# A routed, recurrent, routed block on one core: the second routing scatters its rows into slots, and the recurrence's rotations move to VectorE

## The chip, the cores and the metric

One core of a Trainium2 chip runs the whole program. The metric is the device time of one execution in microseconds, given as the median of several runs. The engines that matter are TensorE (PE, with PEld for its weight loads), VectorE (DVE), ScalarE (ACT), GpSimd (POOL) and the queue of SyncE (SP), which only issues transfers here.

## The reference, cut to what matters

```python
# x: [8, 512, 128] float32, that is T = 4096 tokens of D = 128
def moe(tokens, gate_w, w1, w2):          # E = 8 experts, F = 512, CAP = 160
    probs = softmax(tokens @ gate_w)
    e = argmax(probs)                     # one expert for each token
    pos = rank of the token among those of its expert, in token order
    # tokens with pos >= CAP are dropped: they get 0 from this layer
    out[t] = probs[t, e] * (relu(tokens[t] @ w1[e]) @ w2[e])
x = x + 0.5 * moe(layernorm(x), ...)
u = layernorm(x)                          # per batch: 512 steps of a linear recurrence
Bu = u @ B_w.T
h[t] = ifft(lambda * fft(h[t-1])).real + Bu[t]     # lambda from a_params, |lambda| = 1
x = x + h @ C_w.T + D * u
x = x + 0.5 * moe(layernorm(x), ...)      # same weights, routed anew
```

Token order runs over all batches, so the rank of a token in the second routing is known only once everything ahead of it has been routed.

## The kernel before, in words

The token tiles are 128 rows wide: NT = 32 tiles, TB = 4 of them for each of the NB = 8 batches. The experts have E * CAP = 1280 slots in all, held as NS = 10 tiles of 128 slots. The program has five stages.

1. **First routing** (`mark(0, 0)`, `rank(0, 0)`, `make_hot(0, 0)`, `place(0, 0)`, `index(0)`). VectorE picks the expert of each token and counts within a tile (`mark`). TensorE turns counts into ranks over all tokens (`rank`). VectorE makes slot numbers from them and one-hot tables of each slot number's two parts (`make_hot`). TensorE multiplies these tables, so that each slot gets the number of its token (`place`), and VectorE writes the list `tok` (`index`). GpSimd then gathers rows of x by `tok`, ten indirect transfers (`gather`, L317).
2. **Experts** (`slots(0)`). The steps are written out by hand in `pe_steps`, `dve_steps` and `act_steps`: i takes a slot tile in, u and d are the up and down products of an expert, o turns a row tile back, and x are small products that do nothing but run TensorE. GpSimd scatters the ten result tiles to `x1_dram` (`scatter`, L326).
3. **Recurrence** (L697 to L786 on VectorE, L972 to L1036 on TensorE). SP loads x1 batch by batch. A batch is split into groups of four steps. For batch b: VectorE's `stats` and `shift` and ScalarE's `deviation` and `normalise` make u, TensorE turns it (`turn_u`, L977), ScalarE copies it out (`copy_uT`), and TensorE sums each group (`group_sums`, L986). Then the sums are rotated back, added up along time and rotated forth. The rotation needs both halves of the 128 state rows exchanged, and before the change three engines share it: ScalarE copies the halves crosswise (`turned_part`, L419 and L420), GpSimd multiplies them (vb, L339), VectorE multiplies the plain part (va, L722), adds up (`carry`, z, L730) and makes zs in two half-height instructions (L734), while GpSimd makes zc (L344). `turn_forth` adds both to `state`. TensorE's `within_groups` and `read_out` make y, and VectorE's `add_back` and `gate_back` make x2 and its gate logits. The order on TensorE in turn i is `group_sums(i)`, `turn_u(i + 1)`, `read_out(i - 1)`, `within_groups(i)`.
4. **Second routing**, in three pieces of 3, 3 and 2 batches. The first piece's work stands within the recurrence, from turn 3 on, and the rest after it. SP stores x2 to `out` batch by batch (L278). When `index(1)` has written `tok`, and all stores have landed, GpSimd gathers rows of `out` by it.
5. **Experts again** (`slots(1)`), with the same steps, and ten scatters to `out`.

Engines meet through semaphores, each engine runs its own instructions in order, and a wait holds up everything behind it on that engine.

## Time and profile before

| | |
|---|---|
| runs | 176.22, 178.87, 179.49 us, median 178.87 |
| profiled execution, first to last instruction (span) | 175.4 us |
| the profiled execution's own time beside its span | not listed apart; the lowest of the runs is 0.8 us above the span |
| TensorE | 140.6 us busy (80%), mean granted clock 0.913 |
| VectorE | 89.4 us (51%) |
| ScalarE | 58.1 us (33%) |
| GpSimd | 52.8 us (30%), 80 instructions |
| stage 1, to the first gather | 0 to 27.8 us |
| stage 2, to the first statistics on x1 | 27.8 to 65.7 us |
| stage 3, to the last turn's `gate_back` | 65.7 to 120.0 us |
| stage 4, to the first gather's issue | 120.0 to 136.8 us |
| stage 5, to the end of the span | 136.8 to 175.4 us |

Busy shares are averages over these stages. The rows further down are of four kinds: the chain of waits (what released what, followed back from the end), timelines (start in us, length in us, engine, line, operation, tiles, and in square brackets the idle time ahead of it and who ended that), rows of one source line (how many, and the least, median and greatest length in ns), and windows (busy time of each engine in a stretch, and PEclk, the granted TensorE clock, where 1.00 is 2.4 GHz and 0.50 is 1.2 GHz). A timeline merges neighbouring instructions of one line: x4 means four.

### The profile page before, as it was taken

The page shows a single profiled execution, that of the slowest core. Times are in us where ns is not written, and L with a number is a line of the kernel's source. Part 1 is how long each engine was busy: PE and PEld are TensorE (multiplying, and loading weights), DVE is VectorE, ACT ScalarE, POOL GpSimd, SP SyncE. Part 2 cuts the span into 40 slices and gives each one's busy share as a digit, 9 for nine tenths or more (in the row PEclk, how much of TensorE's full clock was granted, in tenths as well). Part 3 has the DMA queues.
Part 4 walks back from the last instruction along what each step waited for, and adds up shares of the span by engine and source line. Part 5 has one row for each costly group of instructions (what it writes and reads, how often), then busy time and mean ns, then how long its engine had stood idle before and what let it go on. Part 6 is the DMA issues. An engine that isn't in the chain of part 4 may idle for free.

```text
span 175.4 us, 2538 instructions
## 1 busy us (share of the span) xinstructions
PE 140.6 (80%) x791; PEld 108.6 (62%) x791; DVE 89.4 (51%) x396; ACT 58.1 (33%) x144; POOL 52.8 (30%) x80
## 2 busy tenths in 40 slices
PE   6879999989999767599669669697169789999930
PEld 3138497489998322488558558586044269999820
DVE  1069763983583206067458588677754134235320
ACT  3421414554734003753643642610000021483200
POOL 2700005772067700022112112210000677105771
PEclk9997897999999999879999999999656965999996
DMA  4999990111011149000110110111010111000110
GB/s 133 330 366 359 371 551 19 57 48 30 0 36 45 62 133 336 28 2 0 60 60 0 64 60 0 62 60 64 0 60 0 30 45 51 23 4 28 49 45 30
DMA packets 11308, 16.21 MB, mean 92 GB/s; under 512 B 1664, under 2 KB 6272, under 8 KB 11264
## 3 DMA queue, kind: packets, MB, share of 16 engines
q1 hardware_dynamic: 9504, 13.11, 21.3%
q0 software_dynamic: 1280, 2.62, 5.0%
q10 hardware_dynamic: 512, 0.33, 0.7%
q8 instruction: 6, 0.10, 0.2%
q14 instruction: 6, 0.05, 0.1%
HBM read 12.65 MB, written 5.51 MB: 104 GB/s over the span
## 4 chain that ended last, share of the span: by engine, by line
PE 41%; DVE 22%; issue 11%; ACT 8%; DMA 8%; POOL 5%; SPq 1%; POOLq 1%; DVEq 0%; ACTq 0%
PE pair L910 12%; PE pair L921 10%; ACT u L440 5%; PE pair L852 4%; DVE sstat L701 4%; PE pair L879 4%; DMA xt<-x_turned 3%; PE pair L804 3%; PE pair L899 2%; DVE x L748 2%; POOL zc L344 2%; DVE smv L706 2%; DVE z L730 2%; DMA x<-x_scratch 2%; DMA xg<-out,tok 1%
## 5 line engine op out<-in xcount | busy, mean ns | idle before, releaser
L804 PE MATMUL pair<-warm_in,ones_bf 128*128 128x512 bf16 x80 | 22.3, 428 | 3.9 <-DMA x<-x_scratch 1.7
L910 PE MATMUL pair<-xcT,w1s 128*128 128x160 f32 x128 | 22.5, 323 | 0.0
L921 PE MATMUL pair<-hT,w2s 128*128 128x160 f32 x128 | 21.4, 312 | 0.8 <-ACT hT L394 0.8
L910 PEld LDWEIGHTS pair<-xcT,w1s 128*128 128x128 f32 x128 | 19.7, 206 | 0.9 <-ACT xcT L386 0.8
L921 PEld LDWEIGHTS pair<-hT,w2s 128*128 128x128 f32 x128 | 18.8, 199 | 1.5 <-ACT hT L394 0.8
L394 ACT ACTIVATE hT<-pair 128x320 f32<-128x320 f32 x32 | 13.7, 435 | 17.1 <-PE pair L910 15.8
L440 ACT ACTIVATE u<-x,snb,srs 128x128 f32<-128x128 f32 x32 | 13.1, 481 | 13.4 <-DVE snb L716 13.4
L804 PEld LDWEIGHTS pair<-warm_in,ones_bf 128*128 128x128 bf16 x80 | 8.3, 110 | 13.9 <-issue 3.3
L317 POOL DMA_INDIRECT xg<-x,tok x10 | 10.2, 1017 | 21.5 <-DVE tok L638 18.8
L317 POOL DMA_INDIRECT xg<-out,tok x10 | 10.1, 1006 | 20.9 <-DVE tok L638 18.2
L339 POOL TENSOR_TENSOR vb<-vq,st 128x128 f32<-128x128 f32 x8 | 3.6, 455 | 39.5 <-ACT vq L420 39.5
L386 ACT COPY xcT<-pair 128x128 f32<-128x128 f32 x20 | 4.9, 266 | 30.0 <-PE pair L894 30.0
L977 PE MATMUL pair<-ce,u 128*128 128x128 f32 x32 | 5.7, 305 | 10.6 <-ACT u L440 10.4
L326 POOL DMA_INDIRECT out<-xnew,tok x10 | 9.9, 985 | 12.4 <-DVE xnew L682 10.5
L326 POOL DMA_INDIRECT x_scratch<-xnew,tok x10 | 9.9, 988 | 11.0 <-DVE xnew L682 9.2
L672 DVE COPY eoT<-pair 128x160 f32<-128x160 f32 x16 | 5.2, 322 | 13.7 <-PE pair L921 13.6
L879 PE MATMUL pair<-hot_tok,hot_place 128*64 128x20 f16 x64 | 7.8, 265 | 5.3 <-DVE hot_place L623 5.3
L879 PEld LDWEIGHTS pair<-hot_tok,hot_place 128*64 128x64 f16 x64 | 7.4, 202 | 7.5 <-DVE hot_place L623 6.6
L977 PEld LDWEIGHTS pair<-ce,u 128*128 128x128 f32 x32 | 3.7, 150 | 12.4 <-ACT u L440 12.4
L645 DVE BATCH_NORM_STATS2 gstat<-xg 128x6 f32<-128x128 f32 x20 | 5.6, 282 | 9.8 <-DMA xg<-out,tok 7.9
L701 DVE BATCH_NORM_STATS2 sstat<-x 128x6 f32<-128x128 f32 x32 | 6.9, 277 | 7.1 <-DMA x<-x_scratch 7.1
L722 DVE TENSOR_TENSOR va<-pair,ct 128x128 f32<-128x128 f32 x8 | 2.3, 291 | 15.9 <-ACT vq L420 15.9
(170 smaller groups left out, 259.7 us busy)
## 6 DMA issues: line engine op xcount, KB each, us to landing
xt<-x_turned SPq DMA_DIRECT2D x8, 256.0 KB, 5.9
w1s<-w SPq DMA_DIRECT2D x2, 1024.0 KB, 7.4
w2s<-w SPq DMA_DIRECT2D x8, 256.0 KB, 6.6
x<-x_scratch SPq DMA_DIRECT2D x8, 256.0 KB, 4.5
out<-x SPq DMA_DIRECT2D x8, 256.0 KB, 2.0
ce<-const_early ACTq DMA_DIRECT2D x1, 318.0 KB, 4.4
cl<-const_late SPq DMA_DIRECT2D x1, 256.0 KB, 5.5
xg<-x,tok POOLq DMA_INDIRECT x10, 2.5
```

The source lines that it names most:

```text
L317: pool.indirect_dma_start(xg[:, j, :], None, (x_rows, out_rows)[n], bass.IndirectOffsetOnAxis(ap=tok[:, j:j + 1], axis=0), bounds_check=T ...
L326: pool.indirect_dma_start((x1_dram, out_rows)[n], bass.IndirectOffsetOnAxis(ap=tok[:, j:j + 1], axis=0), xnew[:, j, :], None, bounds_check ...
L394: nc.scalar.activation(hT[:, e % 2, half * HC:(half + 1) * HC, :], bank[4 + half][:, 0:HC * CAP] .rearrange("p (c s) -> p c s", c=HC), ACT ...
L440: ins = nc.scalar.activation(u[:, b % 2, c, :], x1[:, b * TB + c, :], ACT.Identity, bias=snb[:, b % 2, c:c + 1], scale=srs[:, b % 2, c:c + 1])
L645: link(V.bn_stats(gstat[:, j, :], xg[:, j, :]))
L701: ins = V.bn_stats(sstat[:, b % 2, c, :], x1[:, b * TB + c, :])
L804: M(bank[to][:, :], ones_bf[:, :], warm_in[:, :], start=True, stop=True)
L852: M(bank[e % 2][:, :], center[:, :], w1s[:, e, :], start=True, stop=True).then_inc(w1c_ps, 1)
L879: ins = M(bank[7][0:SW, 0:NSTRIP], hot_place[:, :, t], hot_tok[:, :, t], start=(t == 0), stop=(t == NT - 1))
L910: ins = M(bank[4 + half][:, c * CAP:(c + 1) * CAP], w1s[:, i, ch * P:(ch + 1) * P], xcT[:, i * CAP:(i + 1) * CAP], start=True, stop=True)
L921: ins = M(bank[6 + i % 2][:, 0:CAP], w2s[:, i, c, :], hT[:, i % 2, c, :], start=(c == 0), stop=(c == FC - 1))
L977: ins = nc.tensor.transpose(bank[4][:, c * P:(c + 1) * P], u[:, b % 2, c, :], ident)
```

## The change

For the second routing, `hot` tables, `place`, `index` and `gather` are gone. VectorE writes each token's slot number straight into `slot_u` (`number`), and GpSimd scatters the token rows of x2 into a DRAM buffer with one row for each slot (`push`): 32 indirect transfers of 128 rows, in five pieces of 2, 2, 2, 1 and 1 batches. A row has grown from 128 to 130 numbers: the token's number rides along in column 128. The buffer is filled once, early, from a zeroed tile whose token number is out of range, so that an empty slot's result goes nowhere. When all 32 have landed, SP reads the buffer back into `xs` in four plain transfers. In the recurrence, ScalarE's crosswise copies and GpSimd's two products are gone, and VectorE makes them: two half-height instructions for vb, read from PSUM, and one for zc. On TensorE `read_out(i - 1)` now comes right after `group_sums(i)`, and `within_groups` is cut in two, with `turn_u(i + 1)` between.

```diff
-    PIECES = [[(0, NB)], [(0, 3), (3, 6), (6, NB)]]
+    PIECES = [[(0, NB)], [(0, 2), (2, 4), (4, 6), (6, 7), (7, NB)]]
+    RW = D + 2
+    ARRIVE = [(0, 2), (2, 4), (4, 7), (7, NS)]
...
 @block.sync
             sp.dma_start(x1_dram, x_rows).then_inc(d_fill, 16)
+            sp.wait_ge(empty_set, 1)
+            sp.dma_start(slots_dram.rearrange("(j p) c -> p j c", p=P), xs[:, :, :]).then_inc(d_empty, 16)
...
-                sp.dma_start(tiles(out_rows, b), x2[:, b * TB:(b + 1) * TB, :]).then_inc(d_out, 16)
+                sp.dma_start(tiles(out_rows, b), x2[:, b * TB:(b + 1) * TB, 0:D]).then_inc(d_out, 16)
+            sp.wait_ge(d_push, 16 * NT)
+            for g, (j0, j1) in enumerate(ARRIVE):
+                sp.dma_start(xs[:, j0:j1, :], slots_dram[j0 * P:j1 * P, :].rearrange("(j p) c -> p j c", p=P))\
+                    .then_inc(d_slots[g], 16)
...
 @block.gpsimd
             nc.gpsimd.memset(xg[:, :, :], 0.0).then_inc(pool_set, 1)
+            link(nc.gpsimd.memset(xs[:, :, :], 0.0))
+            nc.gpsimd.memset(xs[:, :, D:D + 1], SKIP).then_inc(empty_set, 1)
+            nc.gpsimd.memset(x2[:, :, D + 1:RW], 0.0)
+            nc.gpsimd.tensor_copy(x2[:, :, D:D + 1], token_no.unsqueeze(2)).then_inc(token_set, 1)
...
+            def push(k):
+                b0, b1 = PIECES[1][k]
+                pool.wait_ge(slotted, k + 1)
+                pool.wait_ge(x2_r, b1)
+                for t in range(b0 * TB, b1 * TB):
+                    pool.indirect_dma_start(slots_dram, bass.IndirectOffsetOnAxis(ap=slot_u[:, t:t + 1], axis=0),
+                                            x2[:, t, :], None,
+                                            bounds_check=SLOTS - 1, oob_is_err=False).then_inc(d_push, 16)
...
-                nc.gpsimd.tensor_tensor(vb[:, :], vq[:, :], st[:, 0:NG], ALU.mult).then_inc(vb_r, 1)
...
-                nc.gpsimd.tensor_tensor(zc[:, :], z[:, 0:NG], ct[:, 0:NG], ALU.mult).then_inc(zc_r, 1)
-            gather(1)
+            for k in range(len(PIECES[1])):
+                push(k)
             scatter(1)
...
 @block.scalar
-                nc.scalar.copy(vq[0:P // 2, :], v[P // 2:P, :])
-                nc.scalar.copy(vq[P // 2:P, :], v[0:P // 2, :]).then_inc(vq_sb, 1)
...
 @block.vector
             def turn_back(b):
-                dve.wait_ge(vq_sb, b + 1)
-                V.tensor_tensor(va[:, :], bank[5][:, 0:NG], ct[:, 0:NG], ALU.mult).then_inc(va_r, 1)
+                dve.wait_ge(v_ps, b + 1)
+                V.tensor_tensor(va[:, :], bank[5][:, 0:NG], ct[:, 0:NG], ALU.mult)
+                for src, dst in halves:
+                    ins = V.tensor_tensor(vb[dst, :], bank[5][src, 0:NG], st[src, 0:NG], ALU.mult)
+                ins.then_inc(va_r, 1)
...
+                for src, dst in halves:
+                    V.tensor_tensor(zs[dst, :], z[src, 0:NG], st[src, 0:NG], ALU.mult)
+                V.tensor_tensor(zc[:, :], z[:, 0:NG], ct[:, 0:NG], ALU.mult).then_inc(zs_r, 1)
...
-                if i == ROUTE_FROM + 2:
-                    make_hot(1, 0, (True, False))
-                if i == ROUTE_FROM + 3:
-                    make_hot(1, 0, (False, True))
-            mark(1, 1)
+                if i in (2, 4, 6):
+                    mark(1, i // 2 - 1)
+                if i in (3, 5, 7):
+                    number(1, i // 2 - 1, slot_u).then_inc(slotted, 1)
+            mark(1, 3)
             gate_back(NB - 1)
-            mark(1, 2)
+            number(1, 3, slot_u).then_inc(slotted, 1)
+            mark(1, 4)
             add_back(NB - 1)
-            make_hot(1, 1)
-            make_hot(1, 2)
-            index(1)
+            number(1, 4, slot_u).then_inc(slotted, 1)
             slots(1)
...
 @block.tensor
                 group_sums(i)
+                if i >= 1:
+                    read_out(i - 1)
+                within_pairs(i)
                 if i + 1 < NB:
                     turn_u(i + 1)
-                if i >= 1:
-                    read_out(i - 1)
-                within_groups(i)
...
+                within_rest(i)
+                if i in (3, 5, 7):
+                    rank(1, i // 2 - 1)
             read_out(NB - 1)
-            place(1, 1)
-            rank(1, 2)
-            keep_warm(8, 0)
-            place(1, 2)
-            keep_warm(16, 0)
+            rank(1, 3)
+            rank(1, 4)
+            keep_warm(12, 0)
+            pe.wait_ge(slotted, len(PIECES[1]))
+            keep_warm(12, 0)
+            pe.wait_ge(d_push, 16 * NT)
+            keep_warm(4, 0)
             slots(1)
```

`number` is the first part of the old `make_hot`, up to the slot number. `scatter(1)` takes its token numbers from `tok_s`, which VectorE copies out of column 128 of `xs` during `slots(1)`.

## Rows read from the trace of the kernel before

**Rows 1.** Chain of waits, a recurrence turn and the second experts' start: start, us, what

```profile
97.33 1.25 ACT u L440 x3
...
140.84 0.33 PE pair L894
```

**Rows 2.** Timeline of VectorE, the second and the fourth turn of the recurrence

```profile
79.80 0.29 DVE L722 TENSOR_TENSOR va<-pair,ct 128x128 f32<-128x128 f32 x1 [2.27 <-ACT vq L420]
...
92.71 0.29 DVE L722 TENSOR_TENSOR va<-pair,ct 128x128 f32<-128x128 f32 x1 [2.27 <-ACT vq L420]
92.92 0.86 DVE L701 BATCH_NORM_STATS2 sstat<-x 128x6 f32<-128x128 f32 x4
...
94.54 0.75 DVE L734 TENSOR_TENSOR zs<-z,st 64x128 f32<-64x128 f32 x2
95.32 0.29 DVE L743 TENSOR_TENSOR state<-zc,zs 128x128 f32<-128x128 f32 x1
...
96.73 0.16 DVE L716 SCALAR_TENSOR_TENSOR snb<-smv,srs 128x4 f32<-128x4 f32 x1
```

**Rows 3.** Source line 734 (ns min/median/max), and GpSimd's timeline in the same turn

```profile
L734 DVE TENSOR_TENSOR zs<-z,st x16: 285/368/453, 76.2 to 118.4; 64x128 f32<-64x128 f32 x16
...
94.58 0.56 POOL L344 TENSOR_TENSOR zc<-z,ct 128x128 f32<-128x128 f32 x1 [1.37 <-DVE z L730]
```

**Rows 4.** Timeline of VectorE, routing of a piece that is 8 tiles wide

```profile
124.03 0.22 DVE L540 TENSOR_REDUCE top<-lgs 128x8 f32<-128x64 f32 x1
...
125.70 0.67 DVE L748 TENSOR_TENSOR x<-pair,x 128x512 f32<-128x512 f32 x1
...
130.69 0.22 DVE L604 TENSOR_TENSOR own_count<-pair,chosen 128x64 f32<-128x64 f32 x1 [1.95 <-PE pair L871]
...
131.52 0.17 DVE L611 SCALAR_TENSOR_TENSOR slot_i<-slot_f,over 128x8 int16<-128x8 f32 x1
```

**Rows 5.** Timeline of TensorE, first group sums, and one turn later on

```profile
72.27 1.16 PE L986 MATMUL pair<-uT,vt 128*128 128x128 f32 x8 [0.68 <-ACT uT L427]
...
92.18 0.66 PE L977 MATMUL pair<-ce,u 128*128 128x128 f32 x4 [1.64 <-ACT u L440]
...
95.94 1.05 PE L986 MATMUL pair<-uT,vt 128*128 128x128 f32 x8
```

**Rows 6.** Windows: PE, PEld, DVE, ACT, POOL busy (instructions), PEclk, DMA share, GB/s

```profile
76.00:77.00 1.00, 1.00 (x5) 0.77 (x4) 0.92 (x4) 0.16 (x1) 0.56 (x1) 0.64 0.03 8
```

**Rows 7.** Source lines 326 and 317, GpSimd's indirect transfers (ns min/median/max)

```profile
L326 POOL DMA_INDIRECT x_scratch<-xnew,tok x10: 980/982/1015, 49.0 to 60.6; - x10
DMA to landing us min/median/max: 2.2/2.2/3.3
...
L317 POOL DMA_INDIRECT xg<-out,tok x10: 992/997/1083, 136.8 to 148.6; - x10
```

**Rows 8.** Chain of waits, the first load of x1 by SP

```profile
62.97 2.74 DMA x<-x_scratch
```

**Rows 9.** Timeline of TensorE: warm-up products, first expert product, last transposes

```profile
130.47 3.60 PE L804 MATMUL pair<-warm_in,ones_bf 128*128 128x512 bf16 x8
...
141.52 2.48 PE L910 MATMUL pair<-xcT,w1s 128*128 128x160 f32 x8
...
167.98 0.44 PE L930 MATMUL pair<-ce,eoT 128*128 128x128 f32 x2 [0.42 <-DVE eoT L672]
```

**Rows 10.** Windows, ahead of the second experts and within them

```profile
141.00:142.00 1.00, 1.00 (x5) 0.58 (x4) 0.30 (x2) 0.27 (x1) 0.83 (x1) 0.79 0.21 66
...
148.00:149.00 1.00, 1.00 (x9) 1.00 (x7) 0.51 (x3) 0.44 (x1) 0.69 (x2) 0.80 0.02 4
```

**Rows 11.** Timeline of GpSimd, early in the program

```profile
7.23 1.16 POOL L303 MEMSET xg<- 128x1280 f32 x1
```

**Rows 12.** Timeline of VectorE during the ten gathers of the first experts

```profile
34.23 0.23 DVE L478 TENSOR_SCALAR tmp<-st 128x8 f32<-128x8 f32 x1
...
35.03 0.45 DVE L478 TENSOR_SCALAR tmp<-st 128x16 f32<-128x16 f32 x1
```

More of the change, by code:

```diff
@@ L123, in macaron_moe_ssm_kernel @@
         xg = sb("xg", [P, NS, D])
+        xs = sb("xs", [P, NS, RW])
+        tok_s = sb("tok_s", [P, NS], U32)
         xcT = sb("xcT", [P, SLOTS])
@@ L189, in macaron_moe_ssm_kernel @@
         d_scatter = sem("d_scatter")
+        d_empty, d_push = sem("d_empty"), sem("d_push")
+        d_slots = [sem(f"d_slots{g}") for g in range(len(ARRIVE))]
         d_out = sem("d_out")
@@ L203, in piece, with arrival @@
             return n * len(PIECES[0]) + k
-        def hot_parts(n, k):
-            t0, t1 = (b * TB for b in PIECES[n][k])
-            return [(t0, (t0 + t1) // 2), ((t0 + t1) // 2, t1)] if n == 0 else [(t0, t1)]
-        def parts_before(n, k):
-            return sum(len(hot_parts(m, j)) for m in range(2) for j in range(len(PIECES[m])) if (m, j) < (n, k))
+        HOT_PARTS = [(0, HALF), (HALF, NT)]
+        def arrival(j):
+            return next(g for g, (j0, j1) in enumerate(ARRIVE) if j0 <= j < j1)
         marked, ranked, rank_read, hot, placed, indexed = (sem(n) for n in ("marked", "ranked", "rank_read", "hot",
                                                                             "placed", "indexed"))
+        empty_set, token_set, slotted, tok_r = (sem(n) for n in ("empty_set", "token_set", "slotted", "tok_r"))
         w1c_ps, w1c_sb = sem("w1c_ps"), sem("w1c_sb")
@@ L556, in plain, with mark @@
                 return a[:, 0:wd * E].rearrange("p (b c e) -> p b c e", c=TB, e=E)
-            def mark(n, k, parts=(True, True)):
+            def mark(n, k):
                 b0, b1 = PIECES[n][k]
@@ L590, in count_up, with number @@
                                      ALU.mult, ALU.add).then_inc(marked, 1)
-            def make_hot(n, k, parts=(True, True)):
+            def number(n, k, into):
                 b0, b1 = PIECES[n][k]
@@ new lines, in number @@
+                rank = bank[RANKS[n]][:, 0:wd * E].rearrange("p (e t) -> p e t", e=E)
+                V.tensor_tensor(own_count[:, :, ts], rank, chosen[n][k][:, :, :], ALU.mult).then_inc(rank_read, 1)
+                dve.wait_ge(rank_read, piece(n, k) + 1)
+                link(V.reduce_sum(count[:, ts], own_count[:, :, ts].rearrange("p e t -> p t e"), axis=AX))
+                V.tensor_scalar(over[:, ts], count[:, ts], CAP + 0.5, SKIP, ALU.is_gt, ALU.mult)
+                link(V.scalar_tensor_tensor(slot_f[:, ts], top_key[:, ts], -float(CAP), count[:, ts],
+                                            ALU.mult, ALU.add))
@@ new lines, in number, with make_hot @@
+                return V.scalar_tensor_tensor(into[:, ts], slot_f[:, ts], float(SLOTS - 1), over[:, ts],
+                                              ALU.add, ALU.add)
+            def make_hot():
+                link(number(0, 0, slot_i))
+                dve.wait_ge(pool_set, 2)
+                dve.wait_ge(place_set, 1)
+                V.tensor_scalar(split_i[:, 0, :], slot_i[:, :], SW - 1, None, ALU.bitwise_and)
+                link(V.tensor_scalar(split_i[:, 1, :], slot_i[:, :], SW.bit_length() - 1, None,
+                                     ALU.logical_shift_right))
+                link(V.tensor_tensor(hot_strip[:, :, :], split_i[:, 1, :].unsqueeze(1).broadcast_to([P, NSTRIP, NT]),
+                                     strip_no[:, :, :], ALU.is_equal))
+                V.tensor_tensor(hot_tok[:, :, :], hot_strip[:, :, :],
+                                token_half[:, :].unsqueeze(1).broadcast_to([P, NSTRIP, NT]), ALU.mult)
+                for t0, t1 in HOT_PARTS:
@@ L682, in slots @@
                         V.scalar_tensor_tensor(xnew[:, i, :], bank[2 + i % 2][:, 0:P],
-                                               gscale[:, i:i + 1], xg[:, i, :], ALU.mult, ALU.add).then_inc(row_sb, 1)
+                                               gscale[:, i:i + 1], rows[:, i, 0:D], ALU.mult, ALU.add).then_inc(row_sb, 1)
+                    if kind == "f" and n == 1:
+                        V.tensor_copy(tok_s[:, :], xs[:, :, D:D + 1].rearrange("p j o -> p (j o)")).then_inc(tok_r, 1)
             V.memset(c1[:, 0:1], 1.0)
@@ L689, in _ @@
             mark(0, 0)
-            make_hot(0, 0)
+            make_hot()
             lagged_inputs()
-            index(0)
+            index()
             outward_tables()
@@ L953, in _ @@
             center_w1(0, E // 2)
-            place(0, 0)
+            place()
             pe.wait_ge(xj_r, 1)
@@ L1002, in within_groups, with within_rest @@
                   skip_group_check=True)
+            def within_rest(b):
+                y = y_pair(b)
+                ut = [uT[:, b % 2, c * P:(c + 1) * P] for c in range(TB)]
                 M(y[:, 1, E:E + 2 * PITCH], ut[1], tab[:, E + PITCH:E + 3 * PITCH], start=False, stop=False,
```

137 lines of the change are left out of this document (40 added, 97 removed).

## The prediction, made before the changed kernel was run

> **What bounds the kernel now.** I read the chain of waits first, then the timelines of each engine in the stretches that it names, then windows for the clock. Up to the first statistics on x1 (65.7 us) the change touches nothing on the chain. In the recurrence the chain goes round through VectorE's statistics and ScalarE's four normalising instructions and its crosswise copies [rows 1]; VectorE stands still for 2.27 us of each turn, waiting for the copy of vq, and a turn takes (92.71 - 79.80) / 2 = 6.46 us [rows 2]. Between 120.0 and 136.8 us it is routing: counting, one-hot tables, `place`, `index`, in which VectorE, TensorE and GpSimd wait for one another. From 140.84 us the chain is TensorE's expert products nearly to the end [rows 1], then three scatters. So the question has two parts: when does TensorE get its slot rows, and how fast is it then.
>
> **The recurrence's turn.** Before, VectorE works from va at 92.71 to the end of snb at 96.89: 4.18 us [rows 2]. Two half-height vb instructions are added. Their nearest row is va, the same operation from the same PSUM bank, which holds VectorE for 0.21 us until the next starts [rows 2]: 0.42 us. A half-height pair from SBUF took 0.75 us in full [rows 2], so that is the upper end. From the start of zs to that of state were 0.78 us [rows 2]. The two zs last 285 and 453 ns, and the long one ran beside GpSimd's zc of 0.56 us [rows 3]. With zc on VectorE I take 0.21 + 0.21 + 0.29 + 0.04 for the semaphore = 0.75 us, a gain of 0.03; the upper end is 0.78 + 0.21. A turn is then 4.18 + 0.42 - 0.03 = 4.57 us, at the most 4.18 + 0.75 + 0.21 = 5.14 us. I take the lower figure, since the instruction that collided with the long zs is gone.
>
> The Trainium skill gives that collision a rule ("SBUF — State Buffer", Who interferes with whom): a VectorE instruction with two SBUF inputs contends with a GpSimd instruction that reads SBUF, and one waits for the other in full. The trace agrees, 453 ns against 285.
>
> The removed waits: ScalarE's two copies leave the loop, and group sums go straight to VectorE. What is late next is either VectorE itself or TensorE. A turn of TensorE is 92.18 to 96.99, 4.8 us [rows 5]. `read_out` and `within_groups` are only moved; since `turn_u(i + 1)` comes before `within_rest(i)`, ScalarE's copy of uT lies beside products and costs nothing. The normalising has a whole turn's time for its 1.65 us, also hidden.
>
> **Routing inside the turns.** `mark` on 8 tiles held VectorE from 124.03 to 125.70, 1.67 us; `number` from 130.69 to 131.69, 1.0 us [rows 4]. They used to hide in the 2.27 us of waiting, and now nothing hides them: VectorE's turn is 4.57 + 1.67 = 6.24 us with a `mark` and 5.57 us with a `number`. The group sums of turn 0 end at 73.43 [rows 5]. Turn 1 I put at 78.8: TensorE's 4.8 us from there, without a read-out but partly at the lower level of its clock [rows 6]. Turn 2 starts at 83.6 (TensorE bounds), turn 3 at 89.8, turn 4 at 95.4, turn 5 at 101.6, turn 6 at 107.2, turn 7 at 112.0, and the third `number` ends at 116. The first piece's slots are thus ready at 95.4 (T0), the second's at 107.2 (T1), the third's at 116 (T2). For two turns beside pushes I add 0.3: T1 = 107.5. The recurrence ends some 4 us earlier than before (120.0); the turn's gain is largely eaten by routing.
>
> **The pushes.** This is the new path. Ten scatters on GpSimd start between 49.0 and 60.6, one each 1.29 us (980 ns and 0.3 between), beside busy and idle VectorE alike [rows 7]. A push has 128 rows too; it moves 520 bytes for 512, and I charge the same. The first piece: 8 x 1.29 = 10.3 us from 95.4, done at 105.7, and GpSimd waits for T1. From there 24 pushes follow without a gap, since T2 = 116 comes before 107.5 + 10.3 = 117.8, and the last two pieces' numbers, about 120 and 123, long before their turn. The last push starts at 107.5 + 23 x 1.29 = 137.2 and lands 2.2 us later [rows 7] at 139.4. Then SP, which has waited for all 32, issues the loads. The nearest row is 2.74 us for the first 256 KB of x1 [rows 8]; for the first 133 KB I take 2.3 us: rows are there at 141.7 to 141.8. Behind SP's wait there is nothing else, behind GpSimd's only the final scatters. Old path: the first row tile came at 139.5 and the second at 140.84 [rows 1], the tenth gather starting at 148.6 [rows 7]. So `place`, `index` and gathers (120 to 139.5) are exchanged for a train of scatters that ends just as late.
>
> **The experts.** Two transposes of 0.33 [rows 1] and three warm products of 0.43 us at half clock [rows 9] put the first expert product at 141.8 + 1.95 = 143.7; before it was 141.52. From there TensorE needed 26.9 us until 168.42 [rows 9]. It hardly waited for gathers, so their being all there gives nothing. The clock fell to half in the window at 141 and was back in that at 148 [rows 10], 6.9 us. TensorE will have stood idle before the rows come again, from some 127 to 139.4, so I let it run at half for as long after the rows' arrival, to 148.7: 5.0 us of product time instead of 6.9, which saves 0.95. The last transposes end at 143.7 + 25.95 = 169.65, 1.2 us later than before. The tail (three scatters) is the same; the copy of `tok_s` is a VectorE instruction beside products.
>
> **Costed at nothing.** GpSimd's new memsets and copy (about one and a half times the 1.16 us of the one for xg) start at 8.4 us [rows 11], and its next duty is the first gather at 27.8; its `eye_gate` copies move 1.7 us later, and VectorE needs them only once it has written the index. If that cover were gone it would cost those 1.7 us. The filling of the buffer (0.67 MB, 2.6 times the 256 KB that took 2.74 us at the most [rows 8]) follows the weights and the filling of `x1_dram` in SP's queue, beside `center_w1` and the first gathers; uncovered it would delay these by some 3 us at the most, which I leave to the range. SP's stores of x2 in 512-byte pieces are waited for only by `scatter(1)`.
>
> **Sum.** 175.4 + 1.2 = 176.6 us of span. The profile's own execution isn't listed apart; its span is 0.8 below the lowest run and 3.5 below the median. Carried over to the median: 178.87 + 1.2 = 180.1 us. About 2% (3.6 us) is what a measurement of this kernel can tell from no change.
>
> **Rivals.**
> 1. *Slower turns.* The upper ends hold: 5.14 us a turn. Turn 1 to T1 has five turns; that is 0.3 + 4 x 0.57 = 2.6 us on T1, and the train of pushes carries it whole to the end: 182.7. For it speaks that ports were seen to collide [rows 3] and that GpSimd is now busy beside five turns; against it, that its indirect transfers left VectorE's short operations mostly alone. Chance 0.20.
> 2. *Slower pushes.* Place: GpSimd's 24 pushes from T1, beside a VectorE that now hardly rests. One VectorE operation beside a gather took 0.45 us where a narrower one took 0.23 [rows 12]; if each push loses that 0.22 too, the train is 24 x 0.22 = 5.3 us longer: 185.4. It decides from 0.10 us a push on (spacing above 1.39). Against: 980 to 1015 ns in all ten scatters [rows 7]. Chance 0.14.
> 3. *The train starts earlier and the clock holds.* If turns with routing stay near TensorE's 4.8 us, so that T1 is at or before 105.7, the pushes run without a gap from T0: last start 95.4 + 31 x 1.29 = 135.4, rows at 140.0, first product 1.0 us after at full clock, and 26.9 - 3.45 = 23.45 us of products: 164.5 against 168.4, so 175.0. For it: four warm products stand directly ahead; against: VectorE's sum. Chance 0.20.
>
> The Trainium skill ("SBUF — State Buffer", SBUF: two separate sides) has a rule that speaks for the second rival: descriptors that GpSimd writes wait while VectorE runs a copy in its two-port mode, 3100 ns where 620 were usual. The recurrence has no such copy between SBUF tiles, and no run here shows a figure of that size.
>
> **How the numbers follow.** The forecast has 0.46 (0.44 within 2%, 0.02 slower). Rival 1: 0.08 within, 0.12 slower. Rival 2: 0.14 slower. Rival 3: 0.17 faster, 0.03 within. Faster 0.17, same 0.55, slower 0.28. The forecast's own range is 177.5 to 182 (clock back 5 us earlier or 2 us later, load 2.0 to 2.7 us). The whole range, 174.8 to 184.2, takes in rivals 1 and 3 and half of 2.
>
> **What would show it.** A turn's length of 5.6 to 6.2 us with no wait of VectorE for vq, TensorE idle per turn; pushes 1.29 us apart with one gap before the second piece; last push near 137 and first row tile near 141.8; half clock at the start of the second experts; no wait of TensorE for slot tiles after the first. Wrong would be: GpSimd waiting for `slotted` more than once, a spacing other than 1.29, T1 off by more than 2 us, or loads of the buffer that take over 3 us.

## The result, and the profile after

The changed kernel took 181.48 us, the median of 6 runs (179.79 to 184.50), against 177.93 us for the kernel before in 6 runs. The ratio is 1.022, with a 95% interval of 1.017 to 1.028: it is slower, clear of noise, and whether by more than 2% stays open. Medians, here and below, are of all runs, and ratios are of each kernel's fast runs alone, those within 1.5% of its fastest (here their medians are 180.29 and 176.35 us, 3.94 us apart). The forecast was 180.1 us within 174.8 to 184.2, with "no change" as the likeliest, so the time lies inside the range and 1.4 us above the point. The profiled execution took 184.14 us, at the upper end of its runs, with a span of 182.3 us; the quickest took 179.79 us with 178.0. So a comparison of the two profiles shows 6.9 us where the medians show 3.55 to 3.94, and one has to find out which part of it is the change.

The page after, with the rows that answer to those of before:

```profile
span 182.3 us, 2511 instructions
PE 141.1 (77%) x771; PEld 105.1 (58%) x774; DVE 92.9 (51%) x422; ACT 53.7 (29%) x128; POOL 67.7 (37%) x94
...
PEclk9997585899999999659999999997597569999985
...
L349 POOL DMA_INDIRECT slots_scratch<-x,slot_u x32 | 31.5, 984 | 48.3 <-DVE slot_u L605 39.8
```

TensorE (141.1 us) and VectorE (92.9 us) are busy for 77% and 51% of the span, so neither total says what ends last. The 32 pushes are 31.5 us of GpSimd's work. Next, VectorE's timeline after (start, us; the same turn as in [rows 2], then the next va, and two slot numbers):

```profile
88.15 0.28 DVE L725 TENSOR_TENSOR va<-pair,ct 128x128 f32<-128x128 f32 x1
88.44 0.59 DVE L727 TENSOR_TENSOR vb<-pair,st 64x128 f32<-64x128 f32 x2
89.06 0.87 DVE L702 BATCH_NORM_STATS2 sstat<-x 128x6 f32<-128x128 f32 x4
...
90.69 0.58 DVE L736 TENSOR_TENSOR zs<-z,st 64x128 f32<-64x128 f32 x2
91.29 0.29 DVE L737 TENSOR_TENSOR zc<-z,ct 128x128 f32<-128x128 f32 x1
91.61 0.29 DVE L744 TENSOR_TENSOR state<-zc,zs 128x128 f32<-128x128 f32 x1
...
93.02 0.16 DVE L717 SCALAR_TENSOR_TENSOR snb<-smv,srs 128x4 f32<-128x4 f32 x1
93.10 0.21 DVE L543 TENSOR_REDUCE top<-lgs 128x8 f32<-128x64 f32 x1
...
94.77 0.27 DVE L725 TENSOR_TENSOR va<-pair,ct 128x128 f32<-128x128 f32 x1
...
113.14 0.17 DVE L605 SCALAR_TENSOR_TENSOR slot_u<-slot_f,over 128x8 uint32<-128x8 f32 x1
...
128.08 0.16 DVE L605 SCALAR_TENSOR_TENSOR slot_u<-slot_f,over 128x4 uint32<-128x4 f32 x1
```

The wait for vq is gone, and in its place stands the routing: `mark` begins at 93.10, right behind snb, and the next turn starts 6.62 us after this one. That is more than the 6.46 us of before. GpSimd's timeline after:

```profile
101.64 0.97 POOL L349 DMA_INDIRECT slots_scratch<-x,slot_u  x1 [36.78 <-DVE slot_u L605]
...
110.70 0.98 POOL L349 DMA_INDIRECT slots_scratch<-x,slot_u  x1 [0.30 <-issue]
114.08 0.98 POOL L349 DMA_INDIRECT slots_scratch<-x,slot_u  x1 [2.40 <-DVE slot_u L605]
...
143.68 0.98 POOL L349 DMA_INDIRECT slots_scratch<-x,slot_u  x1 [0.30 <-issue]
...
175.94 0.98 POOL L338 DMA_INDIRECT out<-xnew,tok_s  x1 [0.31 <-issue]
```

Eight pushes, one wait of 2.40 us for the second piece's slot numbers, then 24 pushes in 29.6 us (114.08 to 143.68) without a gap. The chain of waits after (start, us, what) takes it from there:

```profile
143.68 2.14 DMA slots_scratch<-x,slot_u
145.83 2.11 DMA xs<-slots_scratch
147.99 0.48 PE pair L890
...
149.78 1.10 PE pair L907 x8
```

The last slot number was written at 128.24, and the rows came at 147.94. No engine that computes held them back in these 20 us: it was GpSimd's queue. VectorE was busy beside the first 11 of the 24 pushes and idle beside the rest.

**Where 6.9 us went.** I set a mark S at the first statistics on x1 (65.73 us before, 68.84 after), since the change touches nothing on the chip ahead of it but three memsets, a copy and a fill. In us:

| stretch | before | after | after - before |
|---|---|---|---|
| start to S | 65.73 | 68.84 | +3.11 |
| S to the first expert product | 75.79 | 80.77 | +4.98 |
| first expert product to start of last scatter | 29.34 | 26.33 | -3.01 |
| start of last scatter to the end | 4.54 | 6.36 | +1.82 |
| sum | 175.40 | 182.30 | +6.90 |

The first line belongs almost wholly to that execution, not to the change. TensorE's timeline shows it, for eight products before:

```profile
18.37 3.85 PE L852 MATMUL pair<-w1s,center 128*128 128x512 f32 x8
```

and after, with three rows that are used further down:

```profile
18.38 5.98 PE L848 MATMUL pair<-w1s,center 128*128 128x512 f32 x8
...
127.48 7.56 PE L800 MATMUL pair<-warm_in,ones_bf 128*128 128x512 bf16 x23 [0.22 <-issue]
...
145.87 1.89 PE L800 MATMUL pair<-warm_in,ones_bf 128*128 128x512 bf16 x4 [10.82 <-DMA slots_scratch<-x,slot_u]
...
172.96 0.44 PE L927 MATMUL pair<-ce,eoT 128*128 128x128 f32 x2 [0.42 <-DVE eoT L671]
```

The same products at the same time took 2.1 us longer, at half clock (0.50 from 18 to 22 us, where the kernel before had 0.83 and 1.00). Over all the kernels below, S spreads from 65.7 to 69.4 us. It can be late with the old code ahead of it (in e6 below: 6.22 us for these products, S at 69.13) and early with the new (in e10: 3.91 us, 66.42). Pairs with nearly the same clock there leave 0.2 us (e4 against e6) to 0.7 us (e10 against the kernel before) to the memsets and the fill. Without the first line the profiles differ by 3.8 us, which is what the medians say. So everything from here on is counted from S.

### The profile page after: what moved, and what is told of

It is laid out like the page before. It is cut to its first block, busy times and chain, and to the rows that moved or that the text cites. A ratio compares the mean times of both kernels' runs of the same rounds, so it can differ in the third digit from the quotient of the medians.

```text
span 182.3 us, 2511 instructions
## 1 busy us (share of the span) xinstructions
PE 141.1 (77%) x771; PEld 105.1 (58%) x774; DVE 92.9 (51%) x422; ACT 53.7 (29%) x128; POOL 67.7 (37%) x94
## 4 chain that ended last, share of the span: by engine, by line
PE 40%; DVE 28%; issue 9%; DMA 8%; POOL 8%; ACT 2%; SPq 1%; POOLq 1%; DVEq 0%
PE pair L907 10%; PE pair L918 9%; PE pair L848 6%; POOL slots_scratch L349 5%; DVE sstat L702 3%; DMA xt<-x_turned 3%; DVE x L749 3%; PE pair L896 2%; PE pair L876 2%; DVE chosen L554 2%; PE pair L983 2%; DVE vb L727 2%; DVE smv L707 1%; DMA x<-x_scratch 1%; PE pair L800 1%
## 5 line engine op out<-in xcount | busy, mean ns | idle before, releaser
L349 POOL DMA_INDIRECT slots_scratch<-x,slot_u x32 | 31.5, 984 | 48.3 <-DVE slot_u L605 39.8
L800 PE MATMUL pair<-warm_in,ones_bf 128*128 128x512 bf16 x81 | 24.8, 459 | 15.0 <-DMA slots_scratch<-x,slot_u 10.8
L800 PEld LDWEIGHTS pair<-warm_in,ones_bf 128*128 128x128 bf16 x84 | 9.2, 115 | 27.1 <-DMA slots_scratch<-x,slot_u 11.3
L907 PE MATMUL pair<-xcT,w1s 128*128 128x160 f32 x128 | 20.6, 304 | 0.0
L338 POOL DMA_INDIRECT out<-xnew,tok_s x10 | 9.8, 982 | 22.4 <-DVE xnew L681 20.6
L644 DVE BATCH_NORM_STATS2 gstat<-xs 128x6 f32<-128x128 f32 x10 | 2.7, 272 | 19.7 <-DMA xs<-slots_scratch 19.7
L1017 PE MATMUL pair<-gt,state 128*128 128x272 f32 x32 | 9.1, 406 | 2.7 <-DVE state L744 2.7
L848 PE MATMUL pair<-w1s,center 128*128 128x512 f32 x16 | 11.0, 854 | 0.0
L983 PE MATMUL pair<-uT,vt 128*128 128x128 f32 x64 | 9.6, 298 | 0.7 <-ACT uT L431 0.7
L983 PEld LDWEIGHTS pair<-uT,vt 128*128 128x128 f32 x64 | 8.6, 209 | 1.1 <-ACT uT L431 1.1
L1017 PEld LDWEIGHTS pair<-gt,state 128*128 128x128 f32 x32 | 5.4, 190 | 4.0 <-DVE state L744 3.4
```

Source lines behind the costliest of these rows:

```text
L338: pool.indirect_dma_start((x1_dram, out_rows)[n], bass.IndirectOffsetOnAxis(ap=(tok, tok_s)[n][:, j:j + 1], axis=0), xnew[:, j, :], None, ...
L349: pool.indirect_dma_start(slots_dram, bass.IndirectOffsetOnAxis(ap=slot_u[:, t:t + 1], axis=0), x2[:, t, :], None, bounds_check=SLOTS - 1, ...
L800: M(bank[to][:, :], ones_bf[:, :], warm_in[:, :], start=True, stop=True)
L848: M(bank[e % 2][:, :], center[:, :], w1s[:, e, :], start=True, stop=True).then_inc(w1c_ps, 1)
L907: ins = M(bank[4 + half][:, c * CAP:(c + 1) * CAP], w1s[:, i, ch * P:(ch + 1) * P], xcT[:, i * CAP:(i + 1) * CAP], start=True, stop=True)
L983: ins = M(bank[5][:, 0:NG], vt[:, TB - 1 - c, :], uT[:, b % 2, c * P:(c + 1) * P], start=(c == 0), stop=(c == TB - 1))
```

## The experiments

All of them are built on the kernel before (B) or after (A). Times are medians; where no ratio is given there was one run. "Rows" is the first arrival of slot rows at TensorE.

**e1_turns_only: the recurrence's half of the change alone.** B with the turn on VectorE and A's order on TensorE, the old routing and gathers.

```diff
-                nc.scalar.copy(vq[...], v[...])       # x2, on ScalarE
-                nc.gpsimd.tensor_tensor(vb[:, :], vq[:, :], st[:, 0:NG], ALU.mult)
-                nc.gpsimd.tensor_tensor(zc[:, :], z[:, 0:NG], ct[:, 0:NG], ALU.mult)
+                turn_back, carry, within_pairs, within_rest and their order as in A
```

> The kernel before with half of the change: VectorE makes the rotations, read-out ahead; second routing as before (place, index, gathers). Theory (the train of 24 pushes from the second piece's number costs the time, the turns are a small gain): a turn without routing takes 4.97 us as in the changed kernel instead of 6.46, the first piece's routing (some 4.5 us) is no longer hidden, so the recurrence ends 1 to 2 us earlier after its first statistics than the 54.3 us of before: 1 to 2 us faster than before, about 176. Rival (the turns on VectorE are what made it slower): 1 to 4 us slower than before.

Measured: 172.35 against 175.91 us, ratio 0.969 (0.963 to 0.975): 3.1% faster, by the ratio some 5 us, where I had expected 1 to 2. VectorE's timeline:

```profile
86.60 0.28 DVE L702 TENSOR_TENSOR va<-pair,ct 128x128 f32<-128x128 f32 x1
...
91.56 0.28 DVE L702 TENSOR_TENSOR va<-pair,ct 128x128 f32<-128x128 f32 x1
...
121.95 0.26 DVE L736 TENSOR_TENSOR lgu<-pair,ssd 128x16 f32<-128x16 f32 x2 [2.05 <-PE pair L998]
```

A turn without routing takes 4.96 us, not 6.46. The rows came at S + 71.63 here, against S + 73.78 before and S + 79.15 in A. So this half is a gain, and the scatters' half costs 7.5 us of rows on top of it. With 1.8 us more behind the last scatter that makes 9.3 us, and by the ratios it is (1.022 - 0.969) x 177 = 9.4 us. The slow change is two changes, one good and one worse than it. The 2.05 us wait at 121.95 led to e5.

**e2_warm_through: TensorE kept busy until the rows come.** A with more warm products.

```diff
             pe.wait_ge(slotted, len(PIECES[1]))
-            keep_warm(12, 0)
+            keep_warm(58, 0)
             pe.wait_ge(d_push, 16 * NT)
-            keep_warm(4, 0)
+            keep_warm(8, 0)
```

> The changed kernel with TensorE kept busy by warm-up products through the whole wait for the pushes (58 instead of 12 ahead of the wait, 8 instead of 4 behind it). Theory: the clock is at 2.4 GHz when the rows come, and what the half clock cost there, from the rows' arrival to the window in which the clock came back, 1.4 us at half speed, is won: 0.7 to 1.0 us from the rows to the last transposes. Rival (my forecast's 5 us at half clock within the products): 2 us or more.

Measured: 179.45 us. The first product came 1.01 us after the rows (A: 1.62), but from there to the last scatter's start were 26.44 us, as in A (26.33), with the clock at 1.00 in every window of 2 us from 130 to 170 us. The half clock ahead of the second experts is thus worth about 0.5 us in A, less than the 0.7 to 1.0 us expected and far less than the 2 us or more of the rival. In this execution turn 0 ran at full clock, and turn 1 started at S + 11.71 instead of 14.34; that 2.6 us lies ahead of the edit and I don't count it for the edit.

**e3_early_number: the second piece's slot numbers sooner.** A with `number` ahead of `carry` on VectorE and `rank` ahead of `within_rest` on TensorE.

```diff
                     stats(i + 2)
+                if i in (3, 5, 7):
+                    number(1, i // 2 - 1, slot_u).then_inc(slotted, 1)
                 carry(i)
...
-                if i in (3, 5, 7):
-                    number(1, i // 2 - 1, slot_u).then_inc(slotted, 1)
```

> The changed kernel with the slot numbers of the first three pieces made inside turns 3, 5 and 7, right after the statistics and ahead of the scan, instead of at those turns' ends, TensorE ranking right after turn_u. Nothing else moves. Theory (the second piece's slots release a train of 24 scatters without a gap): first push of the second piece, last push and first rows all 2.5 to 3 us earlier, time 2.5 to 3 us below the changed kernel, some 177.5. Rival (the end of the recurrence or TensorE sets the end, the train is covered): within 0.5 us of the changed kernel.

Measured: 182.12 us, ratio to B 1.022 (1.014 to 1.030), the same as A's. Expected were some 177.5 us. GpSimd's timeline:

```profile
111.57 1.04 POOL L349 DMA_INDIRECT slots_scratch<-x,slot_u  x1 [2.32 <-DVE slot_u L605]
...
141.51 0.98 POOL L349 DMA_INDIRECT slots_scratch<-x,slot_u  x1 [0.30 <-issue]
```

From S the second piece starts at 42.27 (A: 45.24), the last push at 72.21 (74.84) and the rows come at 76.67 (79.15): 2.5 us sooner, as the train theory says. The time did not follow. Windows of e3 (busy PE, PEld, DVE, ACT, POOL with instructions, then the granted clock):

```profile
148.00:150.00 2.00, 2.00 (x9) 1.83 (x8) 0.24 (x2) 0.44 (x1) 0.00 (x0) 0.50 0.00 0
150.00:152.00 2.00, 1.62 (x12) 1.41 (x11) 0.01 (x1) 0.59 (x2) 0.00 (x0) 0.99 0.00 0
```

and of A:

```profile
148.00:150.00 2.00, 2.00 (x8) 1.27 (x9) 1.83 (x10) 0.53 (x2) 0.00 (x0) 0.63 0.83 222
150.00:152.00 2.00, 1.58 (x12) 1.32 (x11) 0.08 (x1) 1.03 (x3) 0.00 (x0) 1.00 0.00 0
```

The products began 2.3 us sooner after S and then took 1.1 us longer to the last scatter, at half clock up to 150 us. That accounts for half of the 2.5 us in this pair of profiles: from S to the end e3 is 1.3 us shorter. Why the ratio shows none of that I can't say, the two kernels having been timed against different runs of B, with intervals 2 and 3 us wide. So e3 moves the train as forecast, and its time bears the theory out neither way.

**e4_short_train: eight pushes fewer.** A whose last two pieces (batches 6 and 7) are not pushed, so their tokens get no expert; the waits go by 24 pushes.

```diff
-            for k in range(len(PIECES[1])):
+            for k in range(3):
                 push(k)
```

> The changed kernel without the last 8 of the 32 pushes: the rows of the last two batches never reach their slots. All else, and the experts' work, stays. Theory: 8 x 1.29 = 10.3 us less from the second piece's first push to the rows, all of it in the time: about 170. Rival (the last pieces' numbers, ready 15 us before the last push, or the end of the recurrence set the end): less than 2 us. It also shows whether the stretch between the last transfer's landing and the end of the span (4.5 us, against 2.7 in the kernel before) hangs on the number of indirect transfers (44 here, 52 in the changed kernel, 40 before): then some 3.2 us.

Measured: 173.15 us, ratio 0.984 (0.977 to 0.992). Chain of waits:

```profile
133.92 2.15 DMA slots_scratch<-x,slot_u
136.09 2.27 DMA xs<-slots_scratch
138.40 0.33 PE pair L890
```

The last push starts 10.27 us sooner from S (8 x 1.287 = 10.3), the rows come 10.1 sooner, and from S to the end it is 11.3 us shorter, 0.7 of it in the stretch after the last scatter. From S on, every microsecond of the train is a microsecond of the kernel. The times say the same more weakly: the median is 8.3 us below A's and the ratio 0.038, or 6.7 us, below, but this kernel ran only twice, and in the profiled execution S was late (69.35).

**e5_readout_first: the last read-out ahead of the ranking.** e1, with one line moved on TensorE.

```diff
+            read_out(NB - 1)
             rank(1, 1)
-            read_out(NB - 1)
             place(1, 1)
```

> The run with the turns alone (e1_turns_only), and on TensorE the last read-out moved ahead of the ranking of the second piece, behind which it waited 3 us for VectorE's counts while VectorE then stood idle for 2.05 us. Theory (after the recurrence a serial chain over VectorE and TensorE sets when the gathers start, so what is cut from it comes out in the time): first gather 1.8 to 2.1 us earlier after the first statistics than in e1_turns_only, time some 168.5. Rival (the clock or the gathers cover it): within 0.5 us of e1_turns_only, 170.5.

Measured: 169.91 against 178.87 us, ratio 0.954 (0.946 to 0.963). The first gather starts at S + 65.84 against 67.98 in e1, 2.1 us sooner as forecast. VectorE has its logits at 119.39 without a wait, where in e1 it waited 2.05 us behind a ranking that nobody needed yet.

```profile
119.39 0.23 DVE L736 TENSOR_TENSOR lgu<-pair,ssd 128x16 f32<-128x16 f32 x2
```

**e6_old_order: TensorE in the order of B.** e1, with `turn_u` ahead of the read-out again.

```diff
+                if i + 1 < NB:
+                    turn_u(i + 1)
                 if i >= 1:
                     read_out(i - 1)
                 within_pairs(i)
-                if i + 1 < NB:
-                    turn_u(i + 1)
                 within_rest(i)
```

> e1_turns_only with TensorE's old order of products in a turn: turn_u ahead of the read-out. Theory (VectorE sets the turn's length, TensorE has some slack in it): turns 1 to 5 grow by 0 to 0.3 us each. Rival (the read-out ahead is what shortened the turn): turns of 5.6 us or more without routing, where e1_turns_only has 4.96.

Measured: 176.8 us. TensorE's timeline, and under it the line of VectorE's:

```profile
90.25 0.66 PE L955 MATMUL pair<-ce,u 128*128 128x128 f32 x4 [1.75 <-ACT u L419]
...
94.02 1.05 PE L964 MATMUL pair<-uT,vt 128*128 128x128 f32 x8
```

```profile
95.11 0.29 DVE L702 TENSOR_TENSOR va<-pair,ct 128x128 f32<-128x128 f32 x1 [1.51 <-PE pair L964]
```

TensorE stands 1.75 us waiting for ScalarE's u with the read-out behind it, and VectorE waits 1.51 us in turn. Turn 2 takes 6.56 us (e1: 4.96), turn 1 5.08 (4.97), turn 6 5.27 (4.50), turns 3 to 5 the same: 2.5 us over turns 1 to 6, of which 1.9 are left at the first gather (S + 69.87 for 67.98). I had written that these parts "are only moved" and given them no gain; moved back, they cost. Neither expectation holds as a whole: only turn 2 is longer than 5.6 us, and it grows by far more than 0.3.

**e7_more_sems and e8_more_gathers: why is the stretch after the last scatter longer?** A has seven semaphores more than B and, by the counts of the pages, 22 indirect transfers more (62 for 40; where an expectation counts otherwise, these counts hold). e7 is e1 with seven tiny memsets on GpSimd, each with its own semaphore; e8 is e1 with six further gathers into a tile that nothing reads.

```diff
             gather(0)
+            for j in range(6):                       # e8
+                pool.indirect_dma_start(extra[:, j, :], None, x_rows, ...tok[:, j:j + 1]...)
```

> e1_turns_only with 7 more semaphores in use, as many as the changed kernel has over it, each incremented once by a small memset on GpSimd in its idle time. The stretch from the last scatter's start to the span's end was 4.5 us with 40 indirect transfers, 5.7 with 44 and 6.4 with 52 in the changed kernel's forms. If semaphores are a part of it (0.7 us by a line through these three): 5.2 to 5.3 us. If only the indirect transfers count: 4.5 us.

> e1_turns_only with 6 more indirect gathers into an unused tile, in GpSimd's idle time between the first gathers and the first scatters. If each indirect transfer lengthens the stretch behind the last scatter by 0.09 us (the line through 40, 44 and 52 with a part for semaphores): 5.1 us; if semaphores do it alone: 4.5 us; if 0.15 us each: 5.4 us.

Measured: 170.03 us (e7) and 173.48 us (e8). The page and last scatter of e7, and of e8:

```profile
span 168.2 us, 2500 instructions
...
163.63 0.98 POOL L328 DMA_INDIRECT out<-xnew,tok  x1 [0.30 <-issue]
```

```profile
span 171.7 us, 2505 instructions
...
166.63 0.98 POOL L329 DMA_INDIRECT out<-xnew,tok  x1 [0.30 <-issue]
```

From that start to the end are 4.57 us with the semaphores (e1: 4.56) and 5.07 us with six transfers more: 0.085 us for each. By this line A, with 22 more, should have 4.56 + 1.87 = 6.43, and e4, with 14 more, 5.75; measured are 6.36 and 5.65. The line is drawn from gathers and meets the pushes within 0.1 us. The line holds in the other profiles too: 4.54 to 4.57 us in all seven with 40 transfers, 6.30 to 6.36 in all four with 62.

e7 and e8 also show what in e1's own profile was not its code. First product to last scatter took 26.7 and 26.6 us in them, and 31.37 in e1. TensorE's timeline of e1:

```profile
151.21 0.47 PE L872 MATMUL pair<-ce,xg 128*128 128x128 f32 x1 [1.65 <-DMA xg<-out,tok]
```

The last gather took 4.13 us from its start to landing (2.48 in e7), TensorE stood 1.65 us for its rows, and the clock was 0.50 from 152 to 158 us, where in e7 it stayed at 1.00. The profiles of e5 (4.33 us, a wait of 1.92) and e11 (4.01 us, 1.66) show the same, with 30.0 and 31.4 us. That is how much one profile of such a kernel can mislead. A, whose rows are all there before its first product, had no such wait in any profile: a merit of the scatters that the forecast did not name.

**e9_warm_chain: e5 with warm products in the gaps.** No arithmetic is changed; TensorE does idle products where it would stand, ahead of turn 0, after `turn_u(0)` and around the last ranking.

```diff
-            keep_warm(14, 6)
+            keep_warm(23, 6)
             turn_u(0)
+            keep_warm(2, 6)
...
+            keep_warm(5, 4)
             rank(1, 1)
+            keep_warm(17, 4)
             place(1, 1)
```

> e5_readout_first with TensorE kept busy by warm-up products in the gaps where it stood idle and then ran at half clock: 23 instead of 14 ahead of the first turn_u and 2 behind it, 5 ahead of the ranking of the second piece and 17 behind it. Theory (half the clock in turn 0 costs 2.6 us, as between the runs in which turn 1 started 14.3 and 11.7 us after the first statistics; half the clock in the chain of ranking and placing costs another 1 to 2 us): first gather at 61.5 to 62.5 us after the first statistics instead of 65.8, time some 164 to 166. Rival (VectorE's part of the chain and the gathers cover TensorE's clock): less than 1 us earlier.

Measured: 168.18 against 177.30 us, ratio 0.941 (0.932 to 0.950), where 164 to 166 us were expected. This version beats both kernels. Its page, then its window and group sums in turn 0, and under them e1's:

```profile
span 164.4 us, 2557 instructions
...
PEclk9999579999999999999999999999999999999985
```

```profile
74.00:76.00 2.00, 2.00 (x14) 1.75 (x13) 1.91 (x12) 0.68 (x2) 0.00 (x0) 1.00 0.01 4
...
72.66 1.16 PE L964 MATMUL pair<-uT,vt 128*128 128x128 f32 x8 [0.24 <-ACT uT L406]
```

```profile
74.00:76.00 2.00, 1.86 (x8) 1.86 (x9) 0.00 (x0) 1.63 (x5) 0.00 (x0) 0.50 0.00 0
...
74.14 2.08 PE L964 MATMUL pair<-uT,vt 128*128 128x128 f32 x8 [0.67 <-ACT uT L406]
```

The same eight group sums take 1.16 us at full clock and 2.08 at half. Turn 1 starts at S + 11.72 (e1, e5: 14.33), and the first gather at S + 62.02 (e5: 65.84). The first gather is within the 61.5 to 62.5 expected. After the first expert product it gains nothing on e7 or e8 (27.05 us to the last scatter against 26.7 and 26.6).

**e10_fine_train: the best that I could make of the scatters.** A with e3's edit and the second routing in pieces of one batch from batch 2 on, so that pushes start sooner.

```diff
-    PIECES = [..., [(0, 2), (2, 4), (4, 6), (6, 7), (7, NB)]]
+    PIECES = [..., [(0, 2), (2, 3), (3, 4), (4, 5), (5, 6), (6, 7), (7, NB)]]
```

> The changed kernel with pieces of one batch from the second piece on and the slot numbers made early in the turn, so that the pushes can follow the batches closely. Theory (32 scatters of 1.29 us cannot end much sooner than turns and routing let them start): each turn with mark and number takes some 7.1 us, the last push starts 70 to 71.5 us after the first statistics, against 74.8 in the changed kernel and 72.2 in e3_early_number, and the rows come at 74.5 to 76, still 3 us or more later than by gathers in e1_turns_only (71.6). Rival (the coarse pieces were the fault of the scatter half): rows at 71 us or sooner.

Measured: 177.96 us. GpSimd's timeline, the first push, the 21st, which is the last one that had to wait for numbers, and the last of all:

```profile
95.11 0.98 POOL L349 DMA_INDIRECT slots_scratch<-x,slot_u  x1 [32.71 <-DVE slot_u L605]
...
121.69 1.04 POOL L349 DMA_INDIRECT slots_scratch<-x,slot_u  x1 [0.98 <-DVE slot_u L605]
...
136.03 0.98 POOL L349 DMA_INDIRECT slots_scratch<-x,slot_u  x1 [0.30 <-issue]
```

The last push starts at S + 69.61 and the rows come at S + 74.09, still 2.5 us after e1's gathers (71.63), and 3.7 if one allows for turn 0, which ended 1.24 us sooner here than in e1 and A (turn 1 at S + 13.10). Finer routing makes turns 3 to 6 last 6.2 to 7.4 us (in A 5.3 to 6.7), so it takes from the recurrence what it gives to the train.

**e11_wide_x2: x2 in rows of 130 numbers.** e1 with A's x2 tile, stored in pieces of 512 bytes.

```diff
-        x2 = sb("x2", [P, NT, D])
+        x2 = sb("x2", [P, NT, D + 2])
```

> e1_turns_only with x2's rows 130 numbers apart as in the changed kernel, so that SP stores it in pieces of 512 bytes. It bears on the stretch behind the last scatter, of which 0.77 us in the changed kernel are more than its indirect transfers explain. If the small pieces cause them: 5.3 us instead of 4.55. If not: 4.55 us. Either way the first gather comes at 68.0 us after the first statistics as in e1_turns_only, since the last store lands before the index is written.

Measured: 175.21 us, the last stretch 4.55 us as in e1, the first gather at S + 66.76 with turn 1 at S + 13.10, the rest of the recurrence as in e1. The layout costs nothing in the last stretch. (The 0.77 us of the expectation came from too low a count of transfers; by the count above nothing is left to explain.)

## Why the prediction was right, and where its steps were off

The range held, and the sign of my point forecast (slower by 1.2 us) was right, but the size came about by errors on both sides, and in part it was luck. The likeliest outcome of the forecast was "no change within 2%" (0.55), and "slower" had 0.28; the ratio lies on the border between the two. Its central sentence, that the train of scatters "ends just as late" as the gathers, was wrong: after S the rows came 5.4 us later than before (79.15 for 73.78), of which the forecast had 2.3. That the time still fell 1.4 us from the point is owed to experts that ran 2.2 us quicker than forecast, to a kernel before whose median came out 0.9 us lower in the comparison (177.93 for 178.87), and to the 3.5 us by which I carried the span to the median, where each execution whose span is listed took 1.8 to 2.2 us more than its span.

**The recurrence's turn: right mechanism, too small.** Forecast 4.57 us on VectorE or 4.8 on TensorE, measured 4.97 (S + 14.34 to S + 19.31), inside the bounds to 5.14. Two terms were mis-sized. The vb pair lasts 0.59 us and VectorE goes on 0.62 us after its start, where I had taken 2 x 0.21 from va's start-to-start in [rows 2]; a half-height instruction from PSUM takes as long here as a full one (0.29 us for 0.28), and the two hardly overlap. From zs to state were 0.92 us (90.69 to 91.61), not 0.75. The trace agrees with the rule of the Trainium skill ("SBUF — State Buffer", Who interferes with whom) as far as it goes: without GpSimd's zc beside it no zs lasted long (284 to 288 ns each in all 16), 0.58 us for the pair against 0.75. Rival 1 is thus half right: turns were 0.4 us longer than forecast, not 0.57.

**TensorE's order: the step "only moved" failed.** I gave it no gain, but e6 shows that in e1 the order is worth 2.5 us in the recurrence: with the old one the faster VectorE waits for TensorE. For A this isn't shown. 1.6 of the 2.5 us fall in turn 2, which in A holds a `mark` and lasts 6.62 us anyhow, longer than the 6.56 of e6.

**Turn 0: mis-sized.** I put turn 1 at S + 13.07; it was 14.34. At half clock (0.50 in the window at 76, after; 0.64 in [rows 6]) turn 0 takes 2.6 us more than at full clock (11.7 in e2, e7 and e9). I had taken the clock as a mixture, and from 76 to 80 us it was wholly half. Of the 1.3 us, 1.1 had come by the end of the group sums (S + 8.82 for S + 7.70), which took 2.08 us for the 1.16 of [rows 5].

```profile
76.00:78.00 2.00, 2.00 (x10) 1.87 (x10) 0.29 (x1) 1.07 (x3) 0.00 (x0) 0.50 0.00 0
```

**Routing inside the turns: right.** `mark` adds 1.65 us (6.62 - 4.97) for 1.67 forecast and `number` 0.89 us (5.86 - 4.97) for 1.0. It is no longer hidden, as forecast. With turn 0 it ate more of the recurrence than I thought: the last `gate_back` inside a turn ended at S + 53.3, 1.0 us sooner than before (54.3), where I had forecast 4.

**The second piece: 3.5 us late.** Its first push started at S + 45.24 instead of S + 41.8 (107.5 - 65.73): +1.3 from turn 0, +1.4 from turn 1 to the slot numbers, and +0.8 from the end of the slot numbers (113.31) to the start of the push (114.08), which I had left out, though before the same step took as long from `tok` to the first gather. That step of the prediction is the one that failed by the most.

**The train: right.** Forecast 23 x 1.29 = 29.7 us, measured 29.60, one gap ahead of the second piece, 980 ns each, first beside a busy VectorE and then beside an idle one. Landing took 2.14 us (2.2 forecast), loading 2.11 (2.3). It was closer than it looks: the third piece's numbers were written at 123.05, only some 1.3 us before its first push. Rival 2, slower pushes, is refuted: it wanted a spacing of 1.39 us or more. The rule that spoke for it (the Trainium skill, "SBUF — State Buffer", SBUF: two separate sides) isn't tested by this: VectorE ran no copy between 114 and 144 us. e4 shows that the train was on the path that sets the end, as the forecast held. Rows came 79.15 - 76.1 = 3.1 us later after S than forecast.

**Rival 3, an early train:** T1 was S + 45.2, not S + 40.0, so its condition was never met. That its clock would be full at the first product came close to true: it was 0.63 in the window at 148, full from 150.

**The experts: 2.2 us shorter than forecast.** Forecast 25.95 us from the first product to the last transposes, measured 23.8 (before 26.9). I let the half clock run until 5.0 us after the first product; that came at 149.61 us, and from 150 the clock was full. Part of this is the execution: e1, e7 and e8 took 26.6 to 31.4 us to the last scatter with hardly any difference in code, by the clock and by a late last gather, so one profile alone could not have fixed this term to 2 us.

**The tail: "the same" failed.** 6.36 us for 4.54: the forecast put its growth at nothing. e8 gives a price for indirect transfers in this stretch, 0.085 us each, and with it 22 more come to 1.9 us. What the chip does in that time no run shows. That pushes cost what gathers cost here is borne out by e4: eight pushes fewer took 0.71 us off this stretch, 0.089 each.

The sum: the forecast was +1.2 us of span. The errors are +3.5 (second piece), -0.1 (train), -0.3 (landing and load), -0.3 (from the rows to the first product), -2.2 (experts) and +1.8 (tail), +2.4 together. 1.2 + 2.4 = 3.6, where the profiles from S on differ by 3.8 and the medians by 3.55.

**Costed at nothing** were the new memsets and the fill of the buffer. The pairs above leave 0.2 to 0.7 us ahead of S to them, so the time did not hang on it; no run takes them away by themselves.

What stays open: why e3's 2.5 us did not show in its time beyond the part that the clock took, why the last gather lands late in some executions, and what makes the chip grant half or full clock in turn 0 in executions of one program.

## What to carry to other kernels

When a change does two things, price each by its own: here a gain of 3% and a loss of 5% stood under one diff, and the gain alone, with one more line moved and warm products in the gaps, is 6% faster than the kernel before. Before scattering rows early in place of a gather, count the transfers: here 32 of 1.29 us on one queue, for the gather's ten, are a train of 41 us, and it has to start 41 us before its rows are wanted, whatever the computing engines do. Once an engine stops waiting, look for what was hidden in the wait (the routing here), and look at who is queued behind an instruction that nobody needs yet: `rank` ahead of the last read-out was 2 us for one line.

## What the runs showed of the hardware

- Indirect transfers of 128 rows have a steady price on GpSimd's queue: a scatter some 980 ns and 1.29 us from start to start, of 512 or 520 bytes a row, beside a busy VectorE as beside an idle one; a gather some 1,000 ns and 1.31 us. Each also seems to leave 0.085 us in the stretch after the last scatter, however early it ran (e8 against e1, one run each; 4.5 us with 40 transfers, 5.65 with 54, 6.3 with 62).
- Split in two halves of 64 partitions, a product read from PSUM holds VectorE for 0.31 us a part (288 ns in the median), as long as one on 128 (282 ns).
- The same eight products in the same place took 3.85 us in one execution and 5.98 in another; turn 0 took 2.6 us more at half clock than at full. In e9, with TensorE kept busy, the page's clock row shows no fall between the sixth slice and the end. A single profile of this kernel can be 3 us off from S alone, so stretches are to be compared from a common mark.
